# Moving evictions and splits on VectorE, and one transpose on TensorE, in a two-layer graph attention kernel

## What is computed

```python
x = _layernorm(x + _L0_gnn_ref(x, Wq, bq, Wk, bk, Wv, bv, Wf, bf, adj))
x = _layernorm(x + _L1_gnn_ref(x, adj, W, b, w_src, w_dst, H_w, H_b))
# L0: six heads of 64: softmax(q k^T / 8 + mask) v, then @ Wf + bf
# L1: twelve heads of 32: h = x W; sd = tanh(h) . (w_src, w_dst)
#     p = softmax(mask(leaky(src + dst^T))); f = elu(p h + b)
#     gate = sigmoid(x H_w^T + H_b); gate * f + (1 - gate) * x
```

## Time and profile before

| | us |
|---|---|
| median of 3 runs | 1132.04 (1130.24 to 1132.44) |
| profiled execution | 1132.1 |
| its span, first to last instruction | 1130.2 |
| TensorE busy | 1073.2 (95%) |
| ScalarE busy | 919.4 (81%) |
| VectorE busy | 897.2 (79%) |
| GpSimd busy | 765.2 (68%) |
| mean granted TensorE clock | 0.986 of full speed |

### The profile page before, as it was taken

How to read it: one execution, slowest core, us unless ns; L and a number is a source line. 1 busy time by engine, 2 the same in 40 slices (tenths; PEclk the granted TensorE clock), 3 DMA queues, 4 the chain that set the end, 5 groups by cost and what they waited for, 6 DMA issues and landing times.

```text
span 1130.2 us, 25501 instructions
## 1 busy us (share of the span) xinstructions
PE 1073.2 (95%) x8236; PEld 883.3 (78%) x8236; DVE 897.2 (79%) x1828; ACT 919.4 (81%) x3383; POOL 765.2 (68%) x909
## 2 busy tenths in 40 slices
PE   6889999999999999999999999999999999997774
PEld 5678888888888888878888888888888888786652
DVE  5457878888887888888788888878888887888874
ACT  3348888888888888888888888888888888888874
POOL 1367776676777667677766767776676777667652
PEclk9999999999999999999999999999999999999986
DMA  9101010020101002010100201010020101000000
GB/s 270 56 2 57 15 68 18 8 71 16 64 15 61 26 8 71 16 64 15 62 26 8 71 15 64 15 60 27 8 72 16 64 15 43 16 8 16 16 15 21
DMA packets 25893, 44.66 MB, mean 40 GB/s; under 512 B 2462, under 2 KB 23714, under 8 KB 25762
## 3 DMA queue, kind: packets, MB, share of 16 engines
q1 hardware_dynamic: 23234, 41.91, 10.9%
q10 hardware_dynamic: 2496, 1.12, 0.5%
q0 software_dynamic: 32, 0.00, 0.0%
HBM read 30.43 MB, written 12.58 MB: 38 GB/s over the span
## 4 chain that ended last, share of the span: by engine, by line
PE 57%; POOL 23%; issue 9%; DVE 6%; ACT 3%; DMA 2%; POOLq 0%; ACTq 0%; DVEq 0%
PE ps_b L253 13%; PE ps_d L253 13%; POOL z L964 9%; PE ps_a L253 7%; PE ps_d L459 5%; POOL xT_lo L916 4%; PE ps_a L382 3%; PE ps_s L362 3%; PE ps_s L354 3%; PE ps_d L447 3%; POOL p L991 3%; PE ps_c L469 2%; POOL s L956 2%; POOL thw L999 2%; POOL y L958 2%
## 5 line engine op out<-in xcount | busy, mean ns | idle before, releaser
L583 ACT ACTIVATE z<-z,s 128x128 f32<-128x128 f32 x768 | 297.1, 391 | 1.5 <-DVE s L798 0.9
L964 POOL TENSOR_TENSOR z<-z,mask 128x512 f32<-128x512 f32 x192 | 218.2, 1164 | 0.5 <-ACT z L679 0.5
L583 ACT ACTIVATION_READ_ACCUMULATOR z<-z,s 128x1 f32 x768 | 146.6, 191 | 0.0
L610 ACT ACTIVATE p<-ps_s,s 128x128 f32<-128x128 f32 x384 | 134.7, 378 | 13.1 <-DVE s L776 13.0
L991 POOL TENSOR_TENSOR p<-p,s 128x768 f32<-128x768 f32 x64 | 94.2, 1471 | 61.4 <-DVE s L804 61.4
L459 PE MATMUL ps_d<-ident,z 128*128 128x128 f32 x768 | 118.7, 278 | 9.2 <-ACT z L583 8.2
L953 POOL TENSOR_SCALAR s<-s 128x1 f32<-128x1 f32 x128 | 28.8, 225 | 143.3 <-DVE s L895 131.6
L999 POOL TENSOR_TENSOR thw<-th,w_sd 128x768 f32<-128x768 f32 x64 | 117.4, 1834 | 3.7 <-ACT th L633 3.7
L459 PEld LDWEIGHTS ps_d<-ident,z 128*128 128x128 f32 x768 | 90.6, 143 | 17.6 <-ACT z L583 9.1
L679 ACT ACTIVATE z<-ps_d 128x512 f32<-128x512 f32 x192 | 100.8, 598 | 1.2 <-PE ps_d L447 1.2
L945 POOL TENSOR_TENSOR xb<-xb,bf_all 128x768 f32<-128x768 f32 x32 | 58.6, 1834 | 58.6 <-DVE sd L878 55.5
(11 more groups left out here) (154 smaller groups left out, 3448.5 us busy)
## 6 DMA issues: line engine op xcount, KB each, us to landing
x_cols<-in_xT_dram SPq DMA_DIRECT2D x16, 768.0 KB, 6.4
xb<-in_x_dram SPq DMA_DIRECT2D x16, 768.0 KB, 4.9
out_dram<-y SPq DMA_DIRECT2D x64, 192.0 KB, 1.8
z<-in_L_gnn_Wq_dram SPq DMA_DIRECT2D x1, 576.0 KB, 6.4
p1T<-in_L_gnn_Wk_dram SPq DMA_DIRECT2D x1, 576.0 KB, 8.7
qT<-in_L_gnn_Wv_dram SPq DMA_DIRECT2D x1, 576.0 KB, 11.1
kT<-in_L_gnn_Wf_dram SPq DMA_DIRECT2D x1, 576.0 KB, 13.4
z<-in_L_gnn_W_dram SPq DMA_DIRECT2D x1, 576.0 KB, 11.7
```

Source lines behind the costliest of these rows:

```text
L583: done = act.activation(z[:, a, :], z[:, a, :], ACT.Exp, bias=neg1[:, a:a + 1], accum_out=sum1[:, a:a + 1])
L610: last = act.activation(p0[:, o, i, :], ps_s[:, o, i * N:(i + 1) * N], ACT.Exp, bias=neg0[:, k:k + 1], accum_out=sum0[:, k:k + 1])
L964: pool.tensor_tensor(z[:, 4 * q:4 * q + 4, :], z[:, 4 * q:4 * q + 4, :], mask[:, t, :].unsqueeze(1).broadcast_to([P, 4, N]), ALU.add).then ...
```

## The change

On TensorE turn_sd goes ahead of project_out. On VectorE the eviction of q, k or v goes ahead of p0T's copy, the split of sd goes ahead of ctxT_lo, and the copy of bank 1 to p1T, which ScalarE did, comes behind cols_R.

```diff
# TensorE
                     if gat:
                         project_gate((2,))
+                    if gat:
+                        turn_sd(tl)
                     if att:
                         project_out(ta, g, j, n, (0, 1))
-                    if gat:
-                        turn_sd(tl)
                     if tail:
                         turn_p1(tl - 1, gat, (2,))
# ScalarE
-                    if tail:
-                        turned_p1(tl - 1, 1)
                     if gat:
                         act.wait_ge(S["sd_turned"], tl + 1)
# VectorE
+                    if qkv and j == 0:
+                        evacuate_q(1)
+                    elif qkv and j == 1:
+                        evacuate_k(0)
+                    elif qkv and j == 2:
+                        evacuate_k(2)
+                    elif qkv:
+                        evacuate_v(3)
                     if att:
                         dve.wait_ge(S["p0_turned"], ta + 1)
...
-                    if qkv and j == 0:
-                        evacuate_q(1)
-                    elif qkv and j == 1:
-                        evacuate_k(0)
-                    elif qkv and j == 2:
-                        evacuate_k(2)
-                    elif qkv:
-                        evacuate_v(3)
...
-                    if att:
-                        dve.wait_ge(S["ctx_made"], ta + 1)
-                        lo_part(ctxT, ps_a, slice(0, N), "ctx_hi", ta + 1, "ctx_lo")
                     if gat:
...
                         dve.tensor_copy(sd3[:, :, 2, :], sd_rest[:, 1, :, :]).then_inc(S["sd3_ready"], 1)
+                    if att:
+                        dve.wait_ge(S["ctx_made"], ta + 1)
+                        lo_part(ctxT, ps_a, slice(0, N), "ctx_hi", ta + 1, "ctx_lo")
                     if tail:
                         turned_p1(tt, 0)
...
+                    if tail:
+                        turned_p1(tt, 1)
                     if has_tail(n, j, 2):
                         t2 = tl - 2
```

## The result

The changed kernel took 1136.93 us (median of 8 runs, 1136.39 to 1140.39) against 1132.27 (8 runs, 1130.24 to 1135.0): 1.0042 times the time before, 95% interval 1.0026 to 1.0058. It is slower, by 4.7 us. The profiled execution has a span of 1134.6 us against 1130.2.

What follows compares the result with a forecast made beforehand. TensorE was taken to bound three of four iterations and GpSimd's chain the passage from j = 3 to j = 0. Forecast: 1132.1 + 5.2 (groups) + 2 (start) + 0.6 (last group) = 1139.9 us, range 1130 to 1144.5.

Steps and rivals of the forecast that it cites:

- +5.2 in the 14 groups: Fourteen groups of four iterations, each +0.37 us: 0.05 + 0.44 - 0.06 - 0.06, in all +5.2 us.
- j = 0, +0.44: Iteration j = 0: p0T 0.32 us late, the split held 0.26 by first_norm's last op, out waits 0.73; net +0.44.
- j = 1 and j = 2, -0.06 each: From O, start of p0T's copy: out waits 0.20 us for ctxT_lo, logits' gaps save 0.29, port costs 0.03; net -0.06.
- j = 3 to j = 0, +0.05: x_lo starts earlier, but its second half holds line 891, so GpSimd's second norm starts at O + 8.28: +0.05 us.
- The start, +2: GpSimd's mask quarters meet the split in two early iterations, about 1 us each: +2, bounds 0 and 4.
- The last group, +0.14 a step: Last group, nothing filled: line 891 comes some 0.14 us later in each of four iterations, +0.6.
- The ports don't bite: Rival: line 891 of j = 3 gets its data ahead of x_lo's second half; -10.9 in the groups, 1122 us; chance 0.17.
- Only line 891 is held: Rival: without j = 0's 0.26 us port hold the group is +0.11, giving 1136.2 us; chance 0.22.

Runs made afterwards that it cites:

- norm_waits: Changed kernel; on GpSimd first_norm's last op (in j = 0 and iterations without fills) and the first group's mask quarters wait for the split of sd: 1130.5 us, ratio 0.9982.
- j0_old: Changed kernel with the order of before on TensorE, VectorE and ScalarE where j is 0: 1131.5 us, ratio 0.9991.
- no_copy: Changed kernel, but the copy of bank 1 to p1T stays on ScalarE: 1127.16 us, ratio 0.9947.
- all_but_copy: xlo_early with the copy of bank 1 to p1T left on ScalarE: 1123.42 us, ratio 0.9921.
- xlo_early: Changed kernel; on GpSimd x_lo's first half goes ahead of the product of p in j = 3, first_norm's last op and mask quarters wait for the split: 1119.86 us.
- mask_late: Changed kernel with only the mask quarters of the first group put behind the wait for the split of sd: 1134.33 us, ratio 1.0013.
- part_split: Kernel before with only the split of sd ahead of ctxT_lo and turn_sd ahead of out: 1149.6 us.
- half_waits: Changed kernel, but the second half of x_lo on GpSimd waits for line 891: 1139.38 us, ratio 1.0058.
- xlo_only: Changed kernel with only x_lo's first half moved ahead of the product of p in j = 3, without waits for the split: 1132.09 us, ratio 0.9997.

## Why the prediction was right, and where it was not

The forecast was 1139.9 and slower; it came to 1136.9 and slower. The mechanisms named are there, but the sum came near by luck. Its largest term, +5.2 in the 14 groups, measured -0.3: j = 0's loss was paid back by the step from j = 3 to j = 0, whose term was wrong. What made the profiled execution 4.4 us slower lies outside the groups: 2.0 in the mask quarters, 1.0 in the last group, 1.5 in the clock and 0.3 ahead of the end of the first transposes. The term that was 5.5 too high was covered in part by clock time that nobody forecast and by a last group that cost more than forecast.

- *j = 0, +0.44.* Right in size and in both causes: p0T starts 0.32 late, line 865 stands behind first_norm's op, the step is 16.32 against 15.88. norm_waits splits it into 0.32 of port and the rest. j0_old takes it away.
- *j = 1 and j = 2, -0.06 each.* Measured -0.08 and -0.07. The wait for ctxT_lo at O + 3.86 (I had 3.89) and both gaps closed. My reason for the gap at the third product was half wrong: I counted on ScalarE without its copy, and in j = 1 and j = 2 no_copy all but closes it with the copy (the step is 0.05 longer in all_but_copy than in xlo_early, and 0.21 in j = 3).
- *j = 3 to j = 0, +0.05: this term failed.* It measured -0.27. Line 891 was held as forecast, but I let x_lo run for 3.92 us, the duration of the earlier trace rows. There line 891 had met the first half and got in ahead of the second, whose row alone is this (timeline of before):

```profile
621.26 2.14 POOL L916 TENSOR_TENSOR xT_lo<-x_cols,xT_hi 128x768 fp32r<-128x768 f32 x1
```

The first half took 1.83; where line 891 does not come between them the two take 3.62 together. So GpSimd's second norm came at O + 7.98 and not at 8.28. Fourteen times 0.32 is 4.5 us, more than the whole miss of 3.0.
- *The start, +2.* The two steps with a mask quarter grew by 2.0, and mask_late shows the cause. The profile's start is 3.5 longer, the other 1.5 being the clock (last section).
- *The last group, +0.14 a step.* Measured +0.34. The prediction has only line 891's later start there and names no meeting. But the third op of the split, a cast that starts 0.17 after first_norm's op, is held (0.54 instead of 0.18), and norm_waits, which takes the meeting away, brings the step back to 15.00:

```profile
1047.72 0.68 POOL L958 TENSOR_SCALAR x<-r,s 128x384 f32<-128x384 f32 x1
...
1047.89 0.54 DVE L868 CAST sd<-sd_rest 128x24 bf16<-128x24 f32 x1
```

- *The rivals.* "The ports don't bite" fell: line 891 took 1.58. But its mechanism is what xlo_early does on purpose, and 1122 was near what that gave (1119.9). "Only line 891 is held" gives 1136.2, closest to the measured time, and it is wrong all the same: line 865 is held in j = 0. The right number there would have been for the wrong reason.

## What to carry to other kernels

Ahead of moving an op on VectorE, list the GpSimd ops that read SBUF in its new place, and those that its new time sets off: here the split that came earlier started x_lo earlier, which then held a later op of VectorE. Here a copy moved to an engine with idle time cost 9.8 us by pushing the op behind it into such a meeting, and won 3.6 once the meeting was taken away. A duration read from a row holds only with the neighbours of that row. And a sum that comes near the measured time has to be checked term by term: here the groups' term came to -0.3 instead of +5.2.

## What the runs showed of the hardware

VectorE's casts of 24 columns are held as well as its ops of that size with two SBUF inputs: behind GpSimd's mask op such a cast took up to 1.80 us. Each ends 0.02 to 0.04 after the end of the op that held it; line 891, with 384 columns, ends 0.41 to 0.42 after. The Trainium skill ("SBUF — State Buffer", "Who interferes with whom") says of ops with two SBUF inputs, and of casts in a two-port mode, that they block wholly. The runs agree, though none shows in which mode the casts ran. Which comes first decides: where the cast (571.25) and first_norm's op (571.26) started together in another j = 0 of the changed kernel, the cast took 0.21 and the subtraction behind it was held (0.46).

TensorE's clock differs between executions at the start. It was granted 0.62 of full speed from 50 to 54 us in the profile of the changed kernel (0.50, its lower level of 1.2 GHz, from 50 to 52) and 1.00 in that of before (stretches: length, busy time and instructions per engine, clock, DMA share, GB/s; the first line is of before, the second of the changed kernel):

```profile
50.00:54.00 4.00, 4.00 (x28) 2.98 (x27) 2.15 (x4) 1.35 (x8) 0.00 (x0) 1.00 0.00 0
```

```profile
50.00:54.00 4.00, 4.00 (x22) 2.85 (x21) 1.82 (x4) 0.00 (x0) 0.00 (x0) 0.62 0.00 0
```

The first step took 13.46 instead of 11.97. TensorE had idled ahead of it in both (busy 2.0 and 2.4 of the 4 us from 46 to 50), and in norm_waits, whose clock was 1.00 from 50 to 54, as much as in the changed kernel (busy 1.94), so that idling alone does not decide it. Other kernels had the 13.5 or the 12.0 in no order that follows their edits, which is why a difference of 1.5 us in one profile's start says nothing.

The third step is another matter. It took 19.4 to 19.6 us in part_split, half_waits, j0_old, no_copy and xlo_only, whose granted clock was 0.86 from 72 to 84 us, and 17.8 in the changed kernel, whose clock was 1.00 there. In all six the split meets the mask quarter ahead of ctxT_lo. In the other eight kernels, where it does not, the clock was 1.00 and the step took 16.2 to 17.0. With one profile of each this is no proof, but it may be that the meeting costs some executions 1.8 us more than the 2.0 counted above.
